# First projection of a four-layer kernel: a loop over four chunks becomes a written-out pipeline of eight items

## The reference, cut to what matters

```python
xn = layernorm(x)                       # 2048 tokens x 128
q = (xn  @ Wq.T) -> heads of 8          # 16 heads
k = (ctx @ Wk.T) -> heads of 8
q = rms_norm(q, q_norm_w); k = rms_norm(k, k_norm_w)   # over the 8 features of a head
q = rope(q, theta=32) * 8 ** -0.5;  k = rope(k, theta=1000)
```

## Time and profile before

| | us |
|---|---|
| median of three runs (lowest, highest) | 2948.5 (2945.0, 2949.82) |
| the profiled execution's own time | 2950.04 |
| its span in the trace | 2948.3 |
| mean granted clock of PE | 0.951 of full |
| PE busy | 2681.8 (91%) |
| DVE busy | 2078.4 (70%) |
| ACT busy | 1950.8 (66%) |
| POOL busy | 1638.5 (56%) |

### The profile page before, as it was taken

How to read it: one execution, slowest core, us unless ns; L and a number is a source line. 1 busy time by engine, 2 the same in 40 slices (tenths; PEclk the granted TensorE clock), 3 DMA queues, 4 the chain that set the end, 5 groups by cost and what they waited for, 6 DMA issues and landing times. The chain is left out here.

```text
span 2948.3 us, 69363 instructions
## 1 busy us (share of the span) xinstructions
PE 2681.8 (91%) x27218; PEld 1714.7 (58%) x27218; DVE 2078.4 (70%) x4018; ACT 1950.8 (66%) x5223; POOL 1638.5 (56%) x1893
## 2 busy tenths in 40 slices
PE   5996999999999999999999999998699888976995
PEld 2553766666666666666666666665244335542552
DVE  3674988888888888888888888885355335745763
ACT  3344888888888888888888888887233343544352
POOL 0522877777777777777777777775232004301520
PEclk8798999999999999999999999999799997998896
DMA  2001100010001000100010000000000000000000
GB/s 103 1 2 44 48 16 16 16 54 16 16 16 54 16 16 16 46 24 15 16 47 24 16 16 16 24 16 10 8 1 1 1 0 1 2 1 1 1 2 14
DMA packets 35645, 55.64 MB, mean 19 GB/s; under 512 B 7168, under 2 KB 32640, under 8 KB 33792
## 3 DMA queue, kind: packets, MB, share of 16 engines
q1 hardware_dynamic: 35328, 51.29, 5.7%
HBM read 25.05 MB, written 1.05 MB: 9 GB/s over the span
## 5 line engine op out<-in xcount | busy, mean ns | idle before, releaser
L1161 POOL TENSOR_TENSOR l_qk<-l_ta,l_tb 128x256 f32<-128x256 f32 x768 | 540.4, 738 | 285.2 <-DVE l_tb L1234 285.2
L675 POOL TENSOR_SCALAR qmr<-q_all,cf 128x256 fp32r<-128x256 f32 x128 | 116.0, 925 | 674.6 <-SPq L476 341.4
L707 DVE TENSOR_REDUCE mrow<-ring 128x2 f32<-128x512 f32 x512 | 324.5, 684 | 196.1 <-PE ring L523 183.9
L1057 ACT ACTIVATE l_pr<-st,l_mn 128x128 f32<-128x128 f32 x1152 | 354.9, 383 | 153.0 <-DVE l_mn L1220 153.0
L1177 POOL TENSOR_TENSOR l_qk<-l_qk,l_rn 128x512 f32<-128x512 f32 x384 | 392.6, 1044 | 102.6 <-DVE l_rn L1259 102.6
L1168 POOL TENSOR_TENSOR l_pr<-l_pr,l_rs 128x512 f32<-128x512 f32 x384 | 396.7, 1057 | 12.6 <-DVE l_rs L1249 12.6
L660 ACT ACTIVATE pt<-st 128x512 f32<-128x512 f32 x384 | 200.2, 600 | 288.0 <-PE st L558 288.0
L1238 DVE TENSOR_REDUCE l_sums<-l_sq 128x8 f32<-128x512 f32 x384 | 249.3, 659 | 27.6 <-ACT l_sq L1066 27.4
L548 PE MATMUL st<-qm,k_all 32*128 32x512 f32 x1024 | 222.8, 672 | 0.0
L1220 DVE TENSOR_REDUCE l_mn<-st 128x4 f32<-128x512 f32 x288 | 189.1, 685 | 41.2 <-PE st L918 38.8
L523 PE MATMUL ring<-ktr,qmr 32*128 32x256 f32 x1024 | 198.5, 396 | 13.8 <-POOL qmr L675 11.4
(11 more groups left out here) (232 smaller groups left out, 6438.9 us busy)
## 6 DMA issues: line engine op xcount, KB each, us to landing
l_vm<-l_v SPq DMA_DIRECT2D x192, 96.0 KB, 2.1
l_wa<-in_wa SPq DMA_DIRECT2D x6, 2048.0 KB, 9.4
l_vm<-l_v SPq DMA_DIRECT2D x192, 32.0 KB, 1.9
l_wf<-in_wf SPq DMA_DIRECT2D x6, 580.5 KB, 3.9
w<-in_w SPq DMA_DIRECT2D x1, 2752.0 KB, 15.8
cf<-in_cf SPq DMA_DIRECT2D x1, 1123.0 KB, 17.8
x<-in_xT SPq DMA_DIRECT2D x1, 1024.0 KB, 4.8
ctxT<-in_ctxT SPq DMA_DIRECT2D x1, 1024.0 KB, 8.3
```

The costliest lines, as they stand in the source:

```text
L707: dve.tensor_reduce(mrow[b % 2][:, t, j, 2 * p:2 * p + 2], bank_of(f"R{r}").rearrange("p (h k) -> p h k", h=2), AX.X, ALU.max).then_inc(ri ...
L1057: ins = act.activation(t.pr[:, u, hh, c, tile, :], bank(g, f"R{hh}", k)[:, x * P:(x + 1) * P], ACT.Exp, scale=-1.0, bias=t.mn[:, u, hh, x: ...
L1161: ins = pool.tensor_tensor(halves[0][:, :, x], halves[1][:, :, x], halves[2][:, :, 1 - x], ALU.add)
```

## The change

The loops go. The four chunks' queries and keys become eight items j = 0..7 (j even: queries of chunk j/2; odd: keys), and each engine's sequence is written out with constants for semaphore values. There are three slots for the products, of two banks each: `st` 0 and 1, `st` 2 and 3, `ring` 0 and 1; item j takes slot j mod 3. The means alternate between `ring` bank 2 and `ov`. `rope_sq`, `rope_rs`, t1 and t2 grow from two buffers to three. Each engine does the first half of item j and then the second half of item j - 1. PE's wait for `out_done` is replaced by a wait, from item 3 on, for t2 of item j - 3 (`rotated`). `rotate(j)` is the three operations of L376, L378 and L382 on slot and buffer j mod 3. The arithmetic, and the number of matmuls, activations and vector operations, are the same.

```diff
-    sq, rs, t1, t2 = (tmp(n, [P, 2, C], F32) for n in ("rope_sq", "rope_rs", "rope_t1", "rope_t2"))
-    outs = (q_all, k_all)
+    sq, rs, t1, t2 = (tmp(n, [P, 3, C], F32) for n in ("rope_sq", "rope_rs", "rope_t1", "rope_t2"))
+    sides = (("q", g.y, q_all), ("k", g.ctxT, k_all))
+    slots = ((g.st[:, 0, :], g.st[:, 1, :]), (g.st[:, 2, :], g.st[:, 3, :]), (g.ring[:, 0, :], g.ring[:, 1, :]))
+    means = (g.ring[:, 2, :], g.ov[:, :])
+    items = 8
@@ tensor
-            with pe.Fori(0, 4) as c:
-                for i, (n, src) in enumerate((("q", g.y), ("k", g.ctxT))):
-                    pe.matmul(g.st[:, 2 * i, :], g.wm(n + "0"), src[:, cols(c)], start=True, stop=True)
-                    pe.matmul(g.st[:, 2 * i + 1, :], g.wm(n + "0r"), src[:, cols(c)],
-                              start=True, stop=True).then_inc(filled, 1)
-                for i in range(2):
-                    pe.wait_ge(squared, c * 2 + i + 1)
-                    pe.matmul(g.ring[:, i, :], g.f("headmean"), sq[:, i, :], start=True, stop=True).then_inc(mean_sq, 1)
-                pe.wait_ge(out_done, c * 2 + 2)
+            def products(j):
+                c, i = divmod(j, 2)
+                n, src, _ = sides[i]
+                if j >= 3:
+                    pe.wait_ge(rotated, 2 * (j - 3) + 1)
+                pe.matmul(slots[j % 3][0], g.wm(n + "0"), src[:, cols(c)], start=True, stop=True)
+                pe.matmul(slots[j % 3][1], g.wm(n + "0r"), src[:, cols(c)], start=True, stop=True).then_inc(filled, 1)
+
+            def mean_square(j):
+                pe.wait_ge(squared, j + 1)
+                if j >= 2:
+                    pe.wait_ge(rstd, 2 * (j - 2) + 1)
+                pe.matmul(means[j % 2], g.f("headmean"), sq[:, j % 3, :], start=True, stop=True).then_inc(mean_sq, 1)
+
+            for j in range(items + 1):
+                if j < items:
+                    products(j)
+                if j >= 1:
+                    mean_square(j - 1)
@@ scalar
+            def square(j):
+                act.wait_ge(filled, j + 1)
+                if j >= 3:
+                    act.wait_ge(mean_sq, j - 2)
+                act.activation(sq[:, j % 3, :], slots[j % 3][0], ACT.Square).then_inc(squared, 1)
+
+            def inverse_root(j):
+                act.wait_ge(mean_sq, j + 1)
+                if j >= 3:
+                    act.wait_ge(out_done, j - 2)
+                act.activation(rs[:, j % 3, :], means[j % 2], ACT.Ln, bias=g.f("eps6", 1)).then_inc(rstd, 1)
+                act.wait_ge(rstd, 2 * j + 1)
+                act.activation(rs[:, j % 3, :], rs[:, j % 3, :], ACT.Exp, scale=-0.5).then_inc(rstd, 1)
+
+            for j in range(items + 1):
+                if j < items:
+                    square(j)
+                if j >= 1:
+                    inverse_root(j - 1)
@@ vector
+            def rotate(j):
+                n, u = sides[j % 2][0], j % 3
+                dve.wait_ge(squared, j + 1)
...
+            def normalise(j):
+                c, i = divmod(j, 2)
+                dve.wait_ge(rotated, 2 * j + 2)
+                dve.wait_ge(rstd, 2 * j + 2)
+                dve.tensor_tensor(sides[i][2][:, cols(c)], t1[:, j % 3, :], rs[:, j % 3, :], ALU.mult).then_inc(out_done, 1)
+
+            for j in range(items + 1):
+                if j < items:
+                    rotate(j)
+                if j >= 1:
+                    normalise(j - 1)
```

More of the change, by code:

```diff
@@ L371, in twice @@
                 return g.f(name, SEQ).unsqueeze(1).broadcast_to([P, 2, SEQ])
[L373 to L386, removed]
+            def rotate(j):
+                n, u = sides[j % 2][0], j % 3
+                dve.wait_ge(squared, j + 1)
+                dve.scalar_tensor_tensor(out=per_batch(t1[:, u, :]), in0=per_batch(slots[u][0]),
+                                         scalar=g.vec(n + "n"), in1=twice(n + "cos"), op0=ALU.mult, op1=ALU.mult)
+                dve.scalar_tensor_tensor(out=per_batch(t2[:, u, :]), in0=per_batch(slots[u][1]),
+                                         scalar=g.vec(n + "nr"), in1=twice(n + "sin"),
+                                         op0=ALU.mult, op1=ALU.mult).then_inc(rotated, 1)
+                dve.wait_ge(rotated, 2 * j + 1)
+                dve.tensor_tensor(t1[:, u, :], t1[:, u, :], t2[:, u, :], ALU.add).then_inc(rotated, 1)
```

## The result

| | before | changed |
|---|---|---|
| median of six runs each, us | 2949.57 (2945.0 to 2952.93) | 2934.53 (2929.31 to 2941.15) |
| ratio, 95% interval | | 0.9951 (0.994 to 0.9961) |
| profiled execution, span | 2948.3 | 2932.0 |

The changed kernel is 0.5% faster, 15.0 us by the medians; the prediction was 2933.5.

What follows compares the result with a forecast made beforehand. No engine was the bound: each 10.3 us trip was a chain through PE, ACT and DVE with slow-clock starts. Terms 0.04, 4.44, 21.36, 0.07 and 0.27 give 26.18 us, 15.4 less, hence 2933.5 us, range 2929.5 to 2938.5.

Steps and rivals of the forecast that it cites:

- The block's length: Queries-and-keys block, table load to table load: 26.18 us in place of 41.56, 15.4 us less.
- DVE's pace: In the block, DVE is slowest at 2.67 us per item, 0.10 over PE; eight items take 21.36 us.
- DVE's start: At the block's start, 4.44 us from PE's first matmul to DVE's first operation, paid once at 1.2 GHz.
- The check that gave DVE's second item its squares in time: Block's start: item 2's square done at 33.98 us, DVE ready at 34.4; slack 0.4 us, growing 0.10 per item.
- The clock stays up: In the block, PE's granted clock is about 0.5 for 4 us, then 1.00 until PE's last mean.
- Rivals 1 and 2: In the block, PE's clock drops in between (2936.5 to 2945 us, chance 0.07) or stays at 1.2 GHz (2950.5, 0.03).
- PE's pauses: In the block's DVE-paced pipeline, PE makes a short pause of about 0.1 us per item.
- The loop's price: At the block's ends, the loop's entry cost 0.25 us; without a loop the exit falls from 0.51 to 0.27.
- The gain is kept: In the first cross attention, POOL's one-time 6.8 us delay moves with the block, so the gain is kept.
- 1.5 us "either way": In the first cross attention, PE's clock rise may shift a microsecond or two, changing the time by up to 1.5 us.
- The time: Whole kernel: 2933.5 us predicted, from sums of 2934.7 (profiled execution) and 2933.1 (median of three runs).

Runs made afterwards that it cites:

- written_out: The kernel before with this block's three loops written out and nothing else, same order and waits: 2945.62 us (one run), block 39.18 us.
- warm_serial: written_out with three more PE matmuls after each chunk's two means, while PE waits for the chunk's last result: 2935.08 us, block 35.19 us.
- two_slots: The changed kernel with two product slots instead of three, PE waiting for t2 of item j - 2: 2933.48 us, block 26.00 us.
- no_add: The changed kernel without DVE's addition of t2 to t1: 2936.28 us (one run), block 25.66 us.

## Why the prediction was right, point by point

- *The block's length*: 26.18 forecast, 26.36 measured. DVE's pace 2.67 against 2.65; DVE's start 4.44 after PE's against 4.42. The check that gave DVE's second item its squares in time took PE's start from the trace before; here the clock rose later, and the item came 0.3 us late. That DVE is the bound, by less than 0.1 us, was shown by taking its addition away.
- *The clock stays up*: shown, 0.97 from 29 to 51 us, with the end of the slow start in it. Rivals 1 and 2 are out. What the Trainium skill says of cycling through PSUM banks ("TensorE: Matmul & The Clock Gate", section on psum-queue depth-cycling) did not happen here, but neither did its condition, short pauses of PE: PE made none before the end of its last mean. So this pipeline does not test that rule.
- *PE's pauses*: this step was wrong, without harm. Rivals 1 and 2 took pauses of 0.1 us per item for given; in fact PE runs ahead at its own 2.57 us per item and made none, in eight items. With two slots only its weight loads waited, 0.3 us at most.
- *The loop's price*: mis-attributed, in a sum that came out all the same. The entry (0.25) is the loop's. The exit (0.25) is not: it is there in written_out and in warm_serial as well, 0.53 us in both. It goes with PE's wait for the last result: the kernels without that wait (changed, two_slots, no_add) have 0.28. The profile of PE's queue at the block's end, in written_out and then in the changed kernel (ns min/median/max, first and last start us):

```profile
L339 PEldq COMPARE_BRANCH  x1: 185/185/185, 63.4 to 63.4; - x1
```

```profile
L342 PEldq DRAIN  x1: 1175/1175/1175, 47.1 to 47.1; - x1
```

  With the wait, PE comes to the block's end only at 63.4, after DVE's last result, and is the last to arrive; in the changed kernel it begins to drain at 47.1 and is there long before the others. And each hand-over between chunks held 0.46 us of the loop, which the prediction had within each trip's 10.3 us without naming it; the sum came out all the same, since the hand-overs go too.
- *The gain is kept*: mostly. POOL's delay moved with the block (7.08 us after its opening, 6.88 before). But attention 0 takes 177.7 to 179.0 us in the changed kernel, its repeat and two_slots, against 176.7 to 177.3 in the three kernels with the longer block. Part of that is the clock, before and changed:

```profile
102.00:104.00 2.00, 2.00 (x16) 1.57 (x19) 0.00 (x0) 0.41 (x2) 0.00 (x0) 0.50 0.02 4
104.00:106.00 2.00, 2.00 (x32) 1.21 (x24) 1.64 (x3) 1.69 (x4) 0.00 (x0) 0.98 0.00 0
```

```profile
90.00:92.00 2.00, 2.00 (x21) 0.89 (x20) 1.42 (x3) 1.55 (x4) 0.00 (x0) 0.69 0.00 0
```

  It rose to 2.4 GHz at 104.1, 37.6 us after the block opened, and now at 91.2, 40.1 us after; 2.5 us more at half clock are 1.3 by estimate, and POOL's 0.2 more. I had allowed 1.5 us "either way"; it came out on one side in all of them: 37.6 to 38.8 us after the opening in the three kernels with the longer block, 39.1 to 40.6 in the seven with the shorter one and POOL's late start. Why the shorter block should bring a later rise is not settled.
- *The time*: 15.2 us in the block, less 1.5 to 2 in attention 0, leave 13 to 14; 15.0 and 10.9 by the medians of two sets. That the first set came within some 1 us of the forecast time is partly luck: the loss in attention 0 was made up by stages that nobody touched (in the two profiles, 1.8 us in the local layers and 1.6 in projection 1). The repeat's median, 2939.1, is 5.6 us over the forecast and 0.6 outside its range.

## What to carry to other kernels

A loop in which the producer waits for the consumer's last result pays for three things: the missing overlap (8.8 us here), the producer's clock after each pause (4.7) and the loop's own hand-over (0.46 per trip). Look for what ends the producer's idle time at the head of each trip; two slots were enough to remove it, a third gave nothing. Before keeping an engine warm, look at the block that pays for it.

## What was not expected of the hardware

- POOL's first tensor_scalar starts 6.8 to 8.3 us late, wherever it stands. One small instruction in a block where POOL is idle brought attention 0 from 177.7 to 179.0 us down to 170.7 to 171.7 (three kernels).
- Unchanged stages differ in length from one execution to the next with the moments at which PE's clock changes (25.1 or 30.2 us for projection 1 at a granted clock of 0.93 or 0.74; 172.8 or 176.4 for attention 2). A gain of 5 us in a kernel like this is read from its block, not from the total.
